# Four attention stages of a decoder kernel: TensorE weighs and projects ahead of the first turn, and scores between the two turns

## What is computed

```
q, k, v = x @ Wq, x @ Wk, x @ Wv            # per item: 128 positions, 16 heads of 16
scores  = q @ k.T / sqrt(16)                # + causal mask, or - slope * distance
probs   = softmax(scores)
out     = (probs @ v) @ Wo + bias
x       = layernorm(x + out)
```

## Time and profile before

| | us |
|---|---|
| median of 3 runs | 3097.12 |
| lowest and highest | 3096.05, 3098.53 |
| the profiled execution | 3085.19 |
| its span, first to last instruction | 3083.4 |
| busy in it: PE, DVE, ACT, POOL | 2722.6, 1632.8, 1436.1, 1409.5 |
| stretch of the wide stage | 863 to 1145 |
| of the first causal stage | 1145 to 1330 |
| of the distance stage | 1655 to 1840 |
| of the last causal stage | 2590 to 2780 |

### The profile page before, as it was taken

How to read it: one execution, slowest core, us unless ns; L and a number is a source line. 1 busy time by engine, 2 the same in 40 slices (tenths; PEclk the granted TensorE clock), 3 DMA queues, 4 the chain that set the end, 5 groups by cost and what they waited for, 6 DMA issues and landing times.

```text
span 3083.4 us, 70976 instructions
## 1 busy us (share of the span) xinstructions
PE 2722.6 (88%) x25057; PEld 2121.9 (69%) x25057; DVE 1632.8 (53%) x3568; ACT 1436.1 (47%) x4586; POOL 1409.5 (46%) x1644
## 2 busy tenths in 40 slices
PE   6888888559989979979995889999996997999999
PEld 6777776436756656655664767877874665768888
DVE  4999999564446655561115763333333224555643
ACT  4666665344456657743336862223231334772310
POOL 3777777442356665543335661323232223663320
PEclk8999999779999999979997999999996998999999
DMA  2000000210000000051112020000007111010100
GB/s 83 3 2 3 3 3 2 64 36 1 24 12 17 15 23 1 12 180 42 45 43 78 0 94 8 11 10 7 10 18 252 32 33 54 1 48 29 53 10 20
DMA packets 75147, 106.19 MB, mean 34 GB/s; under 512 B 11024, under 2 KB 54672, under 8 KB 74656
## 3 DMA queue, kind: packets, MB, share of 16 engines
q1 hardware_dynamic: 68960, 86.68, 8.4%
q0 software_dynamic: 5952, 16.26, 1.7%
HBM read 88.50 MB, written 14.42 MB: 33 GB/s over the span
## 4 chain that ended last, share of the span: by engine, by line
PE 54%; POOL 4%; DVE 4%; ACT 3%; issue 3%; SPq 1%; DMA 1%; DVEq 0%; ACTq 0%; POOLq 0%
PE up_ps L2490 5%; PE e_out_ps L2508 5%; PE t_ps L664 4%; PE s_ps L650 3%; PE bank_a L1554 3%; PE bank_b L1554 3%; POOL probs L569 2%; PE up_ps L2484 2%; ACT probs L798 2%; PE bank_a L612 2%; PE bank_d L701 2%; PE frame_ps L1633 2%; PE bank_b L1570 2%; PE bank_d L620 2%; PE bank_a L1570 2%
## 5 line engine op out<-in xcount | busy, mean ns | idle before, releaser
L569 POOL TENSOR_TENSOR probs<-probs,inv 128x512 f32<-128x512 f32 x320 | 328.0, 1039 | 269.0 <-DVE inv L919 268.6
L3410 POOL TENSOR_TENSOR hc<-h,bc 128x1024 f32<-128x1024 f32 x128 | 302.0, 2359 | 115.3 <-DVE h L3682 90.6
L798 ACT ACTIVATE probs<-s_ps,negmax 128x128 f32<-128x128 f32 (+1 forms) x768 | 297.1, 414 | 5.8 <-DVE negmax L879 4.4
L3682 DVE TENSOR_TENSOR_SCAN h<-da,dbu_ps 128x1024 f32<-128x1024 f32 x128 | 292.5, 2285 | 11.4 <-DVE dbu_ps L3694 4.8
L664 PE MATMUL t_ps<-ident,probs 128*128 128x128 f32 x1280 | 207.7, 285 | 58.7 <-POOL probs L569 50.2
L664 PEld LDWEIGHTS t_ps<-ident,probs 128*128 128x128 f32 x1280 | 138.9, 141 | 125.5 <-POOL probs L569 60.3
L3499 PE MATMUL dta_ps<-dt,a_spread 32*128 32x128 f32 x2048 | 157.6, 294 | 64.8 <-ACT da L3629 39.2
L3629 ACT ACTIVATE da<-dta_ps 128x1016 f32<-128x1016 f32 x128 | 130.2, 1017 | 150.0 <-PE dta_ps L3499 149.6
L3499 PEld LDWEIGHTS dta_ps<-dt,a_spread 32*128 32x128 f32 x2048 | 132.2, 195 | 87.5 <-ACT da L3629 39.0
L2414 POOL DMA_INDIRECT expert_rows_out<-y,row_to x62 | 61.1, 986 | 268.8 <-DVE y L2773 138.3
L879 DVE TENSOR_REDUCE negmax<-s_ps 128x4 f32<-128x1024 f32 (+1 forms) x128 | 156.6, 1223 | 45.1 <-PE s_ps L650 43.4
(11 more groups left out here) (511 smaller groups left out, 6750.6 us busy)
## 6 DMA issues: line engine op xcount, KB each, us to landing
cT<-in_ctx_turned SPq DMA_DIRECT2D x32, 256.0 KB, 2.6
w_down<-in_L_ffn_w SPq DMA_DIRECT2D x8, 1024.0 KB, 11.8
w_up<-in_L_ffn_w SPq DMA_DIRECT2D x8, 1024.0 KB, 13.0
c_in<-in_ctx SPq DMA_DIRECT2D x16, 256.0 KB, 3.0
w_gate<-in_L_ffn_w SPq DMA_DIRECT2D x8, 512.0 KB, 6.6
w_up<-in_L_ffn_w SPq DMA_DIRECT2D x8, 512.0 KB, 8.4
w_down<-in_L_ffn_w SPq DMA_DIRECT2D x8, 512.0 KB, 8.6
w_gate<-expert_rows_out SPq DMA_DIRECT2D x8, 512.0 KB, 6.4
```

Of the source, the lines that this page charges most:

```text
L569: pool.tensor_tensor(probs[:, u % 2, i], probs[:, u % 2, i], inv[:, u % 2, HB * i:HB * (i + 1)].unsqueeze(2).broadcast_to([P, HB, W]), ALU ...
L798: last = act.activation(probs[:, u % 2, i, k, :], src, ACT.Exp, bias=negmax[:, u % 2, at], accum_out=sums[:, u % 2, at])
L3410: pool.tensor_tensor(hc[:, s % 4], h[:, s % 2], bc[:, j, 1, :].unsqueeze(1).broadcast_to([P, 2 * G, P]), ALU.mult).then_inc(hc_ready.sem, 1)
L3682: dve.tensor_tensor_scan(flat(h[:, s % 2]), flat(da[:, s % 4]), dbu_ps[s % 2][:, :, :, :].rearrange("p i g t -> p (i g t)"), 0.0, ALU.mult ...
```

## The change

Only PE's `unit` is edited. The new order in a unit is: weigh, projections, first turn, score, second turn, `out` (in all stages), `turn`. No instruction is added or taken away, and no other engine's order changes. The end of a stage (`if not left`, L731) stays as it was.

```diff
             def unit(b, j, first, left):
                 for u in range(NP):
                     turned, weighing = pair_back(b, j, u, 1), pair_back(b, j, u, 2)
-                    if u > 0 or not first:
-                        turn_probs(turned[0], turned[2], 0)
+                    if u > 1 or not first:
+                        weigh(*weighing)
                     if u == 0 and left:
                         project_qk(b + 1, 1 - j)
                     if u == 1 and left:
                         project_v(b + 1, 1 - j)
-                    if u > 1 or not first:
-                        weigh(*weighing)
                     if u > 0 or not first:
-                        turn_probs(turned[0], turned[2], 1)
-                    if alibi and u == OUT and begun_out(b, first):
-                        out(b - BEHIND, j if BEHIND == 2 else 1 - j, *out_after(b, left))
+                        turn_probs(turned[0], turned[2], 0)
                     if u < NP - 1:
                         score(b, j, u + 1)
                     elif left:
                         score(b + 1, 1 - j, 0)
-                    if not alibi and u == OUT and begun_out(b, first):
+                    if u > 0 or not first:
+                        turn_probs(turned[0], turned[2], 1)
+                    if u == OUT and begun_out(b, first):
                         out(b - BEHIND, j if BEHIND == 2 else 1 - j, *out_after(b, left))
                     if u == NP - 1 and left == 2:
                         turn(b + 2, j)
```

## The result

| | before | changed |
|---|---|---|
| median, us | 3097.82 (4 runs) | 3206.81 (4 runs) |
| lowest and highest | 3096.05, 3098.95 | 3203.94, 3209.09 |
| span of the profiled execution | 3083.4 | 3202.8 |
| mean granted TensorE clock in it | 0.944 | 0.939 |

The changed kernel takes 1.0355 times as long, 95% interval 1.0340 to 1.0369: 109.0 us more by the medians.

A forecast was written before the change was run, and what follows sets the result against it. Bound: a ring through ACT, DVE, POOL and PE, with ACT needing PE's first turn. Wide 32, first causal 32, distance 27, last causal 32 make +123; clock +10; on 3085.19 gives 3218, median 12 higher: 3230 us, range 3190 to 3275.

The forecast's parts named there:

- Projection of q and k ahead of the first turn: Unit 0, all stages: the turn queues behind a projection waiting for xT; +2.06, +1.24, +1.6, +1.45 us, 14 times a stage.
- Projection of v ahead of the first turn: Unit 1, narrow stages: the turn queues behind a projection waiting for finish; +1.10, +0.37, +0.88 us, 13 times a stage.
- Wide units 0 to 2, +0.25 an item: Wide stage: weigh waits for DVE's copy of the second turn; +0.25 us for the units together, between -0.4 and +0.8.
- Weigh ahead of the first turn: PE's unit: weigh fills the wait for POOL but waits for DVE's copy; costs 0.1 to 0.2 us in a plain unit.
- Scores ahead of the second turn: PE's unit: row_max's 43.4 us of waits for scores go, but no gain, since exponentials wait for the first turn's copy.
- theory F: Stated for experiment 7: with projections ahead, the score between the turns costs nearly nothing; moving it back gives 3190 to 3210.
- `out` behind the second turn: Distance stage: out ends at about 2.5 us, ahead of finish at 4.39, so the move is free.
- The clock, +10 us: Causal stages: PE idles ahead of project_v 26 times; one in four brings the lower clock, +10 us.
- 1 (the wait of `project_v` is hidden): Unit 1, narrow stages: DVE reaches finish earlier or the bank is free; 31 us less, 3199; chance 0.10.
- 2 (it pays): PE's waits for POOL are filled and scores arrive early, if xT is ready in time; 3054 to 3090; chance 0.05.
- 3 (no change): The turn's matmuls pass the waiting projection on PE, or the stages' ends hide it; 3097; chance 0.03.
- 4 (the lower clock takes hold): Every item of all four stages has a 1.2 GHz stretch on the path; 108 us more, 3330; chance 0.07.

The follow-up runs named there:

- experiment 1: The changed kernel with the projection of q and k behind the first turn again: 3148.41 us, 1.0164 of the kernel before.
- experiment 7: The changed kernel with the score behind the second turn again: 3219.59 us, 1.0380 of the kernel before.
- 4: The kernel before with only weigh moved ahead of the first turn, in all stages: 3086.08 us, ratio 0.9956.
- experiment 3: The changed kernel with both projections behind the first turn: 3119.35 us, 1.0065 of the kernel before.
- Experiments 2: The changed kernel with only the projection of v behind the first turn again: 3173.11 us, 1.0239 of the kernel before.
- 6: The changed kernel with DVE's finish ahead of row_max in the causal stages, PE unedited: 3182.56 us, 1.0263 of the kernel before.

## The prediction against the runs

The sign and the range (3190 to 3275) held; 3230 was 23 us too high. The mechanism, a first turn queued behind projections that wait, holds for the three narrow stages, where putting both projections behind the turn takes away 81 of 82 us. In the wide stage it is only part of what happens, though the size came out near. By its steps:

- **Projection of q and k ahead of the first turn, 89 us.** The chain is as foretold: 6.32 us in the item above for 6.47, 6.74 for 6.90 in the first causal stage, 6.59 for the distance stage's 6.67, 5.68 and 5.75 by turns for 5.74 in the wide one. Each of the causal values is some 0.15 below the forecast. In the narrow stages experiment 1 gave back 53 of the 59 us of these terms. In the wide stage it gave back 4 of 29: the step that failed is taking a unit's lengthening as the price of this one move. The path was right, and with the score behind the second turn the projections do cost 29.2 us there (experiment 7 less 4). But with both projections back behind the turn the stage is still 21.8 us above before (experiment 3), since weigh and score, at +3.5 and nothing in the sum, make its item nearly as long by another way. That the stage's total came out near is in part luck.
- **Projection of v ahead of the first turn, 31 us.** 7.01 us for 7.07, 6.23 for the distance stage's 6.21, `project_v` 4.84 us behind the exponentials (2753.12 less 2748.28) for 4.86. Experiments 2 and 6 took 35 and 30 us away, from its two ends.
- **Wide units 0 to 2, +0.25 an item.** Their waits for DVE's copy are there (71.7 us over the span, 0.74 in the row), but the units 0 and 1 to 2 took 4.82, 3.93 and 3.85 us by the median, for 4.99, 3.95 and 3.90 before. So this was -0.24 an item: 3.4 us less in place of 3.5 more, as long as the score stands between the turns.
- **Weigh ahead of the first turn.** Called nearly free. Alone it is a gain of 12.7 us, 22 in the narrow stages. The rows had it: 50.2 us of waits for POOL and 43.4 for scores.
- **Scores ahead of the second turn.** "The gain isn't had" was right, but the prediction only asked who uses the scores sooner. It never asked who waits for the second turn, which the scores push back: DVE's copy, and with it the bank of the next first turn. Alone this is +49 us. In the changed order it is no price (experiment 7). There the first turn waits for its projections anyway; that this is the reason is argued, and theory F, built on it, did not foresee the gain of 11.7 us. So it was luck that the sum came out right with this term at nothing: it would have been 50 us off for the same edit without the projections.
- **`out` behind the second turn.** Nearly free, as said: the distance stage, the one where it moved, has a loop of 166.3 us with both projections behind the turn, for 167.1 before, or some 164.4 without two drops of the clock. So weigh, score and `out` together cost at most 2 us there; `out` was never moved alone.
- **The clock, +10 us.** Not there on the whole: the mean granted clock is 0.939 for 0.944. The last section has the rows.
- **The sum.** Forecast +123 without the clock; the loops grew by 109.2, the medians by 109.0. The difference is 5 us of the wide stage (27.0 for 32), 7 of the first causal stage (25.2 for 32; the two units' medians, 7.01 and 6.74 for 5.98 and 5.67 before, make 13 x 1.03 + 14 x 1.07 = 28, and the other 3 lie in the first and last items), and 2 of the distance stage (25.3 for 27); the last causal one was met (31.7 for 32). Drops of the clock hide a little in two of these: without its two the distance stage of before would be 2.7 us shorter (28.0 for 27), and without its two the last causal stage of the changed kernel 2.5 (29.2 for 32).
- **The range.** Its upper end doesn't follow from its own terms: 3230 less 10, plus 39 for all 26 gaps and 10 for the wide units, is 3269, not 3275. Nothing hangs on it here.
- **Rivals.** 1 (the wait of `project_v` is hidden): no, 30 to 35 us hang on it. 2 (it pays): no; `xT` came behind the point it needed. 3 (no change): no. The rule of the Trainium skill's "TensorE: Matmul & The Clock Gate" (Step-by-step: what each phase is for) that matmuls keep program order agrees with this case: the first turn never passed a projection that waited, 1.90 us in the row at 2753.12. 4 (the lower clock takes hold): no.

What stays open: why, in the wide stage, the score between the turns costs 12 us without the projections ahead and gains 12 with them; and why the score between the turns costs the first causal stage 11.7 us and the last one 18.1 when it is moved alone. The waits name the mechanism; its share per stage wasn't taken apart, and the distance stage's 10.2 holds the move of `out` as well.

## What to carry to other kernels

An engine's list is a queue: an instruction that other engines wait for shouldn't stand behind one that waits for something late, even if that fills a gap in the profile. Where two steps hand over through one buffer (turn, ACT's copy, turn, DVE's copy), each handover wants one piece of other work beside it, so look at what stands in each of the two gaps before and after an edit; moving a piece from one gap to the other costs, as the weighing in the wide stage (+9.5 us) and the score (+49 us) show. A bundle of moves can hide a gain: one of the moves here was worth 0.8 to 1% on its own, in the stages where something else filled its old place.

## What the runs showed of the hardware

Idle stretches of TensorE of nearly 2 us mostly left its clock alone. The changed kernel idles 1.81 or 1.90 us ahead of `project_v`, by turns, in the items of the first causal stage. The granted clock there, and around the two drops of the last causal stage (window, its length, busy us and instructions of PE, PEld, DVE, ACT and POOL, then the clock):

```profile
2776.00:2780.00 4.00, 2.10 (x25) 1.42 (x24) 2.79 (x6) 3.23 (x15) 2.55 (x4) 0.99 0.00 0
2780.00:2784.00 4.00, 4.00 (x20) 2.64 (x21) 0.98 (x4) 1.29 (x6) 0.59 (x1) 0.58 0.00 0
1240.00:1400.00 160.00, 125.36 (x1290) 93.25 (x1286) 76.18 (x174) 97.68 (x457) 78.77 (x92) 1.00 0.07 27
```

Over 160 us of the first causal stage, with ten such stretches, the clock was full (1.00). In the last causal stage a stretch of 1.90 us was twice followed by a lower one (at 2780 and 2834), here 0.58, near the level of 1.2 GHz, and the projection behind it took 1.97 us in place of 1.13:

```profile
2766.44 1.13 PE L629 MATMUL bank_d<-wv,xT 128*128 128x256 f32 x4 [1.81 <-DVE y L927]
...
2779.78 1.97 PE L629 MATMUL bank_d<-wv,xT 128*128 128x256 f32 x4 [1.90 <-DVE y L927]
```

The kernel before had such a drop after an idle stretch of only 1.29 us, and the changed kernel shows none in its distance stage from 1740 on, behind idle stretches of 0.9 to 1.0 us. So the length of one idle stretch alone didn't decide. I had allowed a drop behind one in four of 26 stretches; there were two, and they cost some 2.5 us (the two units that they hit in the last causal loop took 8.27 and 8.23 us, and the median is 7.01).
